# First stage of an eight-stage kernel: sliding attention by units of four heads on four row tiles, no division of probabilities, inner biases without single-row products

## The reference, cut to what matters

```python
# x: [8, 256, 128]; 64 memory tokens stand ahead of each sequence; 4 heads of 32; window 64
x_in = concatenate([pm, x], axis=1)
q, k, v = heads(x_in @ wq.T), heads(x_in @ wk.T), heads(x_in @ wv.T)
logits = where(mask, einsum('bhqd,bhkd->bhqk', q, k) / sqrt(dh), NEG)
out_swa = heads_back(einsum('bhqk,bhkd->bhqd', softmax(logits), v)) @ wo.T
# one step of gradient descent on an inner two-layer perceptron, towards out_swa
pred = silu(k_flat @ w1.T + b1) @ w2.T + b2
grads = grad(0.5 * sum((pred - v_flat) ** 2))(w1, b1, w2, b2)
upd = (1.0 - alpha) * p - theta * g          # for each of w1, b1, w2, b2
out_mem = mlp(*upd, k_flat)
g1, g2 = sigmoid(out_swa @ lin1.T), sigmoid(out_mem @ lin2.T)
out = (g1 * out_swa + g2 * out_mem)[:, NUM_PM:, :]
```

## Time and profile before

| | |
|---|---|
| three runs | 4354.6, 4357.73 (median), 4358.72 us |
| profiled execution | 4367.45 us, its span 4366.1 us |
| busy share of the span | PE 84%, DVE 68%, PEld 54%, ACT 50%, POOL 35% |
| attention part, 39 to 190 us | 151.0 us: PE busy 146.96, DVE 60.23, ACT 44.12 us |
| granted TensorE clock there | 0.53 of full speed |

### The profile page before, as it was taken

How to read it: one execution, slowest core, us unless ns; L and a number is a source line. 1 busy time by engine, 2 the same in 40 slices (tenths; PEclk the granted TensorE clock), 3 DMA queues, 4 the chain that set the end, 5 groups by cost and what they waited for, 6 DMA issues and landing times.

```text
span 4366.1 us, 77999 instructions
## 1 busy us (share of the span) xinstructions
PE 3662.5 (84%) x28960; PEld 2358.2 (54%) x28960; DVE 2972.8 (68%) x8096; ACT 2197.6 (50%) x5333; POOL 1533.1 (35%) x1394
## 2 busy tenths in 40 slices
PE   7997787672776688967569999999999999999996
PEld 5552454561232355635336666666666666666665
DVE  4333654555578655479767878888888888888874
ACT  2211342131664232248536666666666666666663
POOL 0000000043566100000046555555555555555551
PEclk6597896586998898979879999999999999999997
DMA  1000000063000000000000001000100100100000
GB/s 48 1 1 0 5 1 11 23 176 103 0 1 0 5 2 1 1 26 2 26 13 14 20 14 45 14 20 14 45 17 16 43 16 17 41 17 16 18 15 17
DMA packets 34170, 94.06 MB, mean 22 GB/s; under 512 B 5008, under 2 KB 15120, under 8 KB 32000
## 3 DMA queue, kind: packets, MB, share of 16 engines
q1 hardware_dynamic: 31264, 83.88, 6.6%
q0 software_dynamic: 2528, 5.18, 0.7%
HBM read 52.41 MB, written 5.18 MB: 13 GB/s over the span
## 4 chain that ended last, share of the span: by engine, by line
issue 31%; PE 31%; DVE 23%; ACT 11%; POOL 2%; DMA 1%; POOLq 1%; SPq 0%; ACTq 0%; DVEq 0%
PE psum L395 4%; PE psum L400 4%; PE psum L3101 4%; PE psum L3070 4%; DVE scratch L3202 3%; ACT y L3161 3%; PE psum L3087 2%; PE psum L3043 2%; DVE scratch L3251 2%; PE psum L561 2%; DVE scratch L3204 2%; ACT L3161 1%; ACT L3134 1%; ACT xn L3156 1%; POOL scratch L2526 1%
## 5 line engine op out<-in xcount | busy, mean ns | idle before, releaser
L3357 POOL TENSOR_TENSOR scratch<-scratch 128x512 f32<-128x512 f32 x384 | 489.3, 1274 | 281.1 <-DVE scratch L3205 281.1
L3406 POOL TENSOR_TENSOR x<-x,y 128x640 f32<-128x640 f32 x8 | 23.7, 2959 | 1548.8 <-DVE y L450 1548.8
L3350 POOL TENSOR_TENSOR xn<-y,scratch 128x384 f32<-128x384 f32 x384 | 317.8, 828 | 637.4 <-DVE scratch L3253 637.3
L3151 ACT ACTIVATE y<-psum 128x512 f32<-128x512 f32 x384 | 229.4, 597 | 615.6 <-DVE scratch L3205 615.6
L3101 PE MATMUL psum<-weights,scratch 128*128 128x512 f32 x768 | 421.3, 631 | 51.0 <-ACT y L3151 38.0
L400 PE MATMUL psum<-table,xn 128*128 128x128 f32 x1648 | 273.9, 292 | 213.3 <-DVE xn L450 212.5
L400 PE MATMUL psum<-table,scratch 128*128 128x128 f32 (+1 forms) x2276 | 389.6, 293 | 68.6 <-ACT scratch L3173 32.0
L3161 ACT ACTIVATE y<-psum,scratch 128x96 f32<-128x96 f32 x1536 | 401.8, 354 | 14.3 <-DVE scratch L3265 13.7
L3251 DVE TENSOR_REDUCE scratch<-y 128x4 f32<-128x384 f32 x384 | 211.1, 550 | 262.3 <-ACT y L3161 262.3
L3043 PEld LDWEIGHTS psum<-scratch 64*64 64x64 f32 x6144 | 266.2, 133 | 221.0 <-issue 221.0
L400 PEld LDWEIGHTS psum<-table,scratch 128*128 128x128 f32 (+1 forms) x2276 | 278.3, 150 | 136.9 <-issue 82.9
(11 more groups left out here) (501 smaller groups left out, 8037.1 us busy)
## 6 DMA issues: line engine op xcount, KB each, us to landing
scratch<-scratch SPq DMA_DIRECT2D x96, 256.0 KB, 3.1
scratch<-experts_dram SPq DMA_DIRECT2D x47, 384.0 KB, 4.3
weights<-layer_dram SPq DMA_DIRECT2D x6, 1357.0 KB, 9.1
weights<-layer_dram SPq DMA_DIRECT2D x6, 1356.5 KB, 6.4
scratch<-scratch SPq DMA_DIRECT2D x48, 128.0 KB, 3.0
weights<-gqa_dram SPq DMA_DIRECT2D x2, 1738.5 KB, 9.2
results_dram<-scratch SPq DMA_DIRECT2D x11, 256.0 KB, 4.8
weights<-mamba_dram SPq DMA_DIRECT2D x2, 665.5 KB, 5.5
```

Source lines behind the costliest of these rows:

```text
L3151: nc.scalar.activation(sq[a % 2], RAW, ACT.Square).then_inc(S("squared").up(), 1)
L3350: gtt(probs[t % 2][:, :, P - KB:], E[t % 2], over_keys(small[t % 4][:, 1, :]), ALU.mult).then_inc(S("divided_pool").up(), 1)
L3357: gtt(out, out, sines, ALU.add).then_inc(S("rope_sum").up(), 1)
```

## The change

Attention goes by 17 units, each one tile with all four heads. The scores of the four heads are products on four row tiles of the array (rows 0, 32, 64 and 96), into four banks of their own, issued one behind the other with no wait between them. A helper that other stages use already, `Bench`, hands out six banks in turn and waits until the former user of a bank has been read. The exponentials keep no running sum, and the probabilities are not divided. Instead `pe_values` makes, beside the product with v, a product of the same probabilities with ones, which puts the sum of each row, 32 times over, beside its values; DVE takes the reciprocal of these sums (128x128 out of PSUM) and multiplies the values by it. DVE's and ACT's loops (`dve_attn`, `act_attn`) are written anew around it:

```diff
+    def pe_scores(u):
+        for h in range(HEADS0):
+            bench.wait_free(pe, ("score", 4 * u + h))
+        parts = segments(u)
+        for col, key, width in parts:
+            for h in range(HEADS0):
+                rows = slice(hd * h, hd * h + hd)
+                last = mm(bench.bank(("score", 4 * u + h))[:, col:col + width], q[rows, tile_at(u) * P:tile_at(u) * P + P],
+                          k[rows, key:key + width], start=True, stop=True)
+                if col + width == 2 * P:
+                    last.then_inc(S("scored").up(), 1)
...
+    def pe_values(u):
+
+        pe.wait_ge(S("copied_act"), u)
+        pe.wait_ge(S("copied_dve"), u)
+        pe.wait_ge(S("swa_out"), u - 2)
+        for at, lhs in ((0, lambda h, b: v[:, tile_at(u) if b else before(tile_at(u)), hd * h:hd * h + hd]),
+                        (P, lambda h, b: c("ones")[:, 0:hd])):
+            for b in key_blocks(u):
+                for h in range(HEADS0):
+                    last = mm(sum_bank(u)[hd * h:hd * h + hd, at:at + P], lhs(h, b), turned[u % 2][:, h, b, :],
+                              start=b == key_blocks(u)[0], stop=b == 1, skip_group_check=True)
+        last.then_inc(S("valued").up(), 1)
+
+    def pe_attn(s):
+        if s < NT:
+            pe_scores(s)
+        if 0 <= s - 2 < NT:
+            pe_turn_probs(s - 2)
+        if 0 <= s - 3 < NT:
+            pe_values(s - 3)
+        u = s - 4
+        if 0 <= u < NT:
+            pe.wait_ge(S("gathered"), u)
+            mm(sum_bank(u)[:, 2 * P:3 * P], w("wo"), attn[u % 2], start=True, stop=True).then_inc(S("projected").up(), 1)
...
+    def dve_attn(s):
+        u = s
+        if u < NT:
+            c0, mask = first_col(u), c("windowmem") if u == 0 else c("window")
+            dve.wait_ge(S("turned"), 2 * (u - 3) + 1)
+            dve.wait_ge(S("cleared"), 0)
+            for h in range(HEADS0):
+                dve.wait_ge(S("scored"), 4 * u + h)
+                nc.vector.tensor_tensor_reduce(probs[u % 3][:, h, c0:], bench.bank(("score", 4 * u + h))[:, c0:2 * P], mask[:, c0:],
+                                               -scale, 3.0e38, ALU.add, ALU.min, least[u % 3][:, h:h + 1]).then_inc(S("bounded").up(), 1)
+        u = s - 3
+        if 0 <= u < NT:
+            dve.wait_ge(S("valued"), u)
+            nc.vector.reciprocal(inverse[u % 2], sum_bank(u)[:, P:2 * P]).then_inc(S("inverted").up(), 1)
+            dve.wait_ge(S("inverted"), u)
+            dve.wait_ge(S("projected"), u - 2)
+            tt(attn[u % 2], sum_bank(u)[:, 0:P], inverse[u % 2], ALU.mult).then_inc(S("gathered").up(), 1)
+        u = s - 2
+        if 0 <= u < NT:
+            dve.wait_ge(S("turned"), 2 * u + 1)
+            dve.wait_ge(S("valued"), u - 2)
+            nc.vector.tensor_copy(*out_of_bank(u, 1)).then_inc(S("copied_dve").up(), 1)
```

```diff
-                mm(zb, ones[0:1, :], w("b1")[0:1, :], start=False, stop=True).then_inc(S("z").up(), 1)
+                pe.wait_ge(S("tables"), 0)
+                mm(zb, ones16, bias, start=False, stop=True).then_inc(S("z").up(), 1)
...
-                mm(gb1[0:1, :], ones[:, 0:1], dh[t % 2], **kw)
...
+        pe.wait_ge(S("summed"), NT - 1)
+        for j in range(4):
+            last = mm(gb1[:, j:j + 1], total[:, j * P:j * P + P], ones[:, 0:1], start=True, stop=True)
+        last.then_inc(S("evened").up(), 1)
...
-                    mm(M.bank(j), nw1[:, j * P:j * P + P], xT[:, g * GROUP:(g + 1) * GROUP], start=True, stop=False)
-                    mm(M.bank(j), nb1[0:1, j * P:j * P + P], ones[0:1, 0:1].broadcast_to([1, GROUP]), start=False,
-                       stop=True).then_inc(S("up").up(), 1)
+                    mm(M.bank(j), nw1[:, j * P:j * P + P], xT[:, g * GROUP:(g + 1) * GROUP], start=True, stop=True).then_inc(
+                        S("up").up(), 1)
...
-                    nc.scalar.activation(hid[g % 2][:, j, :], M.bank(j), ACT.Sigmoid).then_inc(S("silu").up(), 1)
+                    nc.scalar.activation(hid[g % 2][:, j, :], M.bank(j), ACT.Sigmoid, bias=nb1[:, j:j + 1]).then_inc(S("silu").up(), 1)
...
+    def dve_bias():
+        b1 = w("b1")
+        nc.vector.memset(bias, 0.0).then_inc(dve.link(), 1)
+        nc.vector.memset(ones16, 1.0).then_inc(dve.link(), 1)
+        nc.vector.tensor_copy(piece, b1).then_inc(dve.link(), 1)
+        dve.settle()
+        nc.vector.tensor_copy(bias[0:1], piece[0:1]).then_inc(dve.link(), 1)
+        tt(rest, b1, piece, ALU.subtract).then_inc(dve.link(), 1)
+        dve.settle()
+        nc.vector.tensor_copy(piece, rest).then_inc(dve.link(), 1)
+        dve.settle()
+        nc.vector.tensor_copy(bias[32:33], piece[32:33]).then_inc(dve.link(), 1)
+        tt(bias[64:65], rest[64:65], piece[64:65], ALU.subtract).then_inc(S("tables").up(), 1)
...
-                    tt(hid[g % 2][:, j, :], M.bank(j), hid[g % 2][:, j, :], ALU.mult).then_inc(S("hid").up(), 1)
+                    stt(hid[g % 2][:, j, :], M.bank(j), nb1[:, j:j + 1], hid[g % 2][:, j, :], ALU.add, ALU.mult).then_inc(
+                        S("hid").up(), 1)
...
+            pool.wait_ge(S("hidden_grad"), t)
+            if t == 0:
+                nc.gpsimd.tensor_copy(total, dh[0]).then_inc(S("summed").up(), 1)
+            else:
+                pool.wait_ge(S("summed"), t - 1)
+                nc.gpsimd.tensor_tensor(total, total, dh[t % 3], ALU.add).then_inc(S("summed").up(), 1)
```

More of the change, by code:

```diff
@@ L677, in act_gather @@
-def act_gather(A, group, out):
-    M, act = A.M, A.M.act
-    act.wait_ge(M.sig("valued"), (group + 1) * A.in_bank - 1)
-    width = 2 * A.in_bank * max(A.dv, 32) // P * P
-    M.nc.scalar.copy(out[:, 0:width], M.bank(A.o_bank)[:, 0:width]).then_inc(M.sig("gathered").up(), 1)
 def stage_titan(M):
```

293 lines of the change are left out of this document (77 added, 216 removed).

## The result

The changed kernel takes 4206.61 us (median of four runs, 4201.4 to 4210.6) and the kernel before 4356.16 us (four runs beside it, 4347.72 to 4358.72): a ratio of 0.966, 95% interval 0.964 to 0.968. The profiled execution took 4201.4 us, its span 4200.1 us. The forecast of 4223 us was 16 us too high.

A forecast was written before the change was run, and what follows sets the result against it. PE was taken to bound attention, gradients and output part; savings of 71, 30 and 34 us sum to 135 us, giving 4232 from the profiled 4367.45 us and 4223 us for runs, range 4200 to 4260.

The forecast's parts named there:

- A: Whole kernel: the main forecast, with attention units at 3.95 us at clock 1.00; 4223 us, by itself 4206 to 4240; chance 0.58.
- rival D: Attention: reciprocal as cheap as a multiplication, so PE's 3.15 to 3.3 us a unit bind; 4214 us; chance 0.06.
- the ring: Attention unit: PE's transposes, values and sums and DVE's reciprocal, multiplication and copy wait in a circle; 3.95 us at 1.00.
- PE bounds all three parts: Attention, gradients, output: PE busy nearly throughout, so PE work taken out counts unless DVE and its handovers come up behind.
- Its start: Attention: first scores and maxima, then 4 us of bias pieces with PE idle, 6 us together; next three steps 13 us.
- Rival B: Attention: clock stays at 0.50, twelve steps at 5.55 instead of 3.95 us and a slower end; 4245 us; chance 0.20.
- The gradients: Gradient steps: b1 product gone, bias product shorter, step from 8.15 to 6.5 us; -30 us.
- The output part: Output part: sixteen bias products gone and clock 1.00 after some 5 us; -34 us, 47 us of 81 left.
- C: Attention: DVE's ring longer through a 1.9 us reciprocal or handovers, unit 5.0 us; 4236, or 4245 with clock returns; chance 0.12.
- E: Gradient step or output part: the shortening is not had because another wait fills it; up to 30 us back, 4253; chance 0.02.
- F: Attention: row and column tiles don't overlap, a unit takes 13.5 us at 0.50; slower, 4373 us; chance 0.02.

The follow-up runs named there:

- e1: Changed kernel with the old gradient, update and output parts, only the attention by units new; ratio 0.978 to the kernel before.
- e2: Kernel before with only the inner parts new (bias pieces, b1's gradient sum on GpSimd, bias in the sigmoid), attention by pairs of heads kept; ratio 0.983 to before.
- e3: Changed kernel with only VectorE's order altered, the copy of the second transposed bank ahead of reciprocal and multiplication; median 4224.86 us, ratio 0.963 to before.
- e8: Changed kernel with the reciprocal of the 128x128 sums made twice on VectorE, one after the other; 4258.79 us, single run.
- e4: Changed kernel with each head's scores begun only when those of the head before have ended; 4307.62 us, single run.
- e7: Changed kernel with the b1 product of ones put back into each of the 17 gradient steps, its result unused; 4260.88 us, single run.
- e6: Kernel before with the output part's one-row bias product turned into one over 128 rows, 127 of them zero; 4368.8 us, output part 55.3 us.

## Why the prediction was right, and its terms

The forecast, 4223 us in 4200 to 4260 and faster, held with 4206.61. Its mechanisms held as well, and its terms erred to the same side: -135 us were summed and the stage gave -155.6. That the time is off by 16 us only is in part luck, since the medians moved by 149.6 us, less than the stage. Nor does the time alone tell A from rival D, whose 4214 us lie nearer; the rows of the ring do.

- **PE bounds all three parts, at half the clock in two of them.** Right. Taking PE's work out shortened each part, and e1 and e2 show that they add. With the ring opened (e3) a unit took 3.05 us with PE busy throughout; 3.15 had been summed for PE alone.
- **The ring of the attention unit.** Right as a mechanism (e8 +0.99 us, e3 -0.62 us a unit); 3.67 us measured, 3.95 predicted. The terms: reciprocal 0.96 busy (predicted 1.03); values and sums 1.02 (1.2), where I stood too far from the lower bound of 0.86; multiplication and copy 0.95 from start to the transposes (0.29 + 0.69 + a handover of 0.1). The busy times that I added include a tail which the next instruction overlaps. Twelve units: 44.0 instead of 47.4.
- **Its start.** The bias pieces took 3.1 us and not 4 (41.03 to 44.16 us), and PE idled for them, as foretold; the third step began at 44.95 us, 45 predicted. The three steps after it took 10.5 us and not 13. The end took 12.5 us, 13 predicted. Together 72.8 instead of 79.4 us: -78 instead of -71.
- **The clock.** Rival B (0.50 throughout) fell: 1.00 from 52 to 106.5 us with eight transposes in each unit. The rule of the Trainium skill, "TensorE: Matmul & The Clock Gate", section "Part 4: PE-mode transpose", that transposes don't engage the full clock, would have made B likelier. The trace disagrees at least in that a third of PE's work as transposes did not keep it from 1.00, and e4, with the same transposes, had 0.61. My argument against B, PE's unbroken work at 0.50, was not a good one: e4 had that too, and stayed at 0.61.
- **The gradients.** -37.3 us with the update, -30 predicted. The b1 product was put at 0.95 us and cost 1.14 with its neighbours (e7: 19.4 us, 16.2 predicted). The bias product was put at 0.35 and takes 0.22 us; with its neighbours the step gained 2.18 - 1.14 = 1.04 us where 0.70 was put, 14.6 us over 14 steps instead of 9.8. GpSimd's sum is hidden, as foretold.
- **The output part.** -40.2 us, -34 predicted. The sixteen products are 14.7 us of it and the clock 25.5 (e6). The working gave the clock too little in the second half of the part, where it had been 0.86 in the mean: 3.5 us were put for it, and 40 us at 0.86 are some 5.6 us longer than at 1.00. The start at 0.50 was taken as some 5 us without a row for it; it was 3.4 us (226.2 to 229.7), which gives 0.8 more. The other 3 us of the miss are not placed.
- **The other rivals.** C (a longer ring) fell with a reciprocal of 0.96 us; e8, with two of them, shows what C would have cost: 4.66 us a unit and 22 to 24 us in all, with the returns to the lower clock that C named. D (a cheap reciprocal, PE alone) fell, since the reciprocal takes 0.96 us against 0.29 for the multiplication, and PE does wait 0.34 or 0.46 us in each unit. E fell, no new wait is in the gradient step. F, the tiles not overlapping, fell by e4: 1.02 against 4.18 us for the row tiles of a unit at 0.50.

What stays open: why the clock turns where it does within a stretch, and whether the rows or the waits keep it down in e4. The 10.4 us behind the stage that the two profiled spans also differ by I take for scatter, by the 15.3 us between two profiles of one chip; this is argued and was not tested by itself.

## What to carry to other kernels

Where TensorE is busy nearly all of the time at half its clock, look at how many rows its products use before looking at their number: here a single row in every second product, and heads of 32 rows one after another, went with half the clock. Four heads on four row tiles, and a bias folded into the activation, took these away, and the clock was 1.00 for most of both parts. When two engines each show a little idle time in every period, follow the ring, and first try the order within one engine's queue: an instruction that others wait for doesn't belong behind one that itself waits.

## What was not expected of the hardware

- How busy PE was did not go with the clock that it was granted. PE busy 15.00 of 15 us went with 0.50 where every second product used one row, and with 1.00 where the same products used 128 rows (before and e6). PE busy 121.98 of 128 us went with 0.61 where products of 32 rows came in turn, and 47.00 of 54.5 us with 1.00 where four such tiles ran side by side (e4 and the changed kernel).
- A product that uses a single row, or a single column of weights, costs its neighbours too, at clock 1.00: the b1 product 1.14 us a step for 0.95 of its own (e7), the bias product 0.20 us beside the 0.83 of its own (before against after, where a product of 96 rows stands in its place).
- DVE's reciprocal of 128x128 out of PSUM takes 0.96 us against 0.29 for a multiplication of that shape; of 128x4 it takes 0.17.
- One program differs by 0.9% in its time between chips, 4356 to 4397 us in the medians, some 30 us of it behind this stage, where profiles showed 3934 to 3944 us on the faster chips and 3960 to 3975 on the slower; equal parts of the first stage agree within 1.3 us between them (attention 151.1 and 150.8, 72.8 and 71.8, gradients 151.0 and 149.9).
